# Attention with x regrouped through HBM for its transposition, values loaded in merged transfers, and the loop over the batches written out

## The reference

```python
x = x + tanh(g_xattn[0]) * xattn(layernorm(x), ctx, Wq, bq, Wk, bk, Wv, bv, Wo, bo)
x = x + tanh(g_ffn[0]) * ffn(layernorm(x), W1, b1, phases, w_real, w_imag, W2, b2)

def xattn(x1, x2, ...):                     # 16 heads, softmax over the 77 rows of the context
    q, k, v = x1 @ Wq.T + bq, x2 @ Wk.T + bk, x2 @ Wv.T + bv
    return softmax(q k^T / sqrt(32)) v  @ Wo.T + bo

def ffn(x, ...):                            # 512 -> 2048 -> 512
    h = x @ W1 + b1
    imag = w_imag * sin(phases + 0.1 * h)
    q = h + (cos(phases) * w_real + sin(phases) * w_imag) * imag * 0.1
    return relu(q) @ W2 + b2
```

## Time and profile before

| | |
|---|---|
| time, median of 3 runs | 2233.33 us (2232.54 to 2234.48) |
| the profiled execution | 2231.39 us, span 2229.6 us, mean granted clock 0.995 |
| TensorE busy | 2185.5 us, 98% |
| VectorE, ScalarE, POOL busy | 1445.7 us (65%), 1213.6 us (54%), 408.0 us (18%) |
| transfers | 169.38 MB in 269170 packets, of which 190928 under 512 B |

### The profile page before, as it was taken

One profiled execution on the slowest core, in us unless ns is written; L12 is line 12 of the kernel. 1 busy time (PEld: TensorE's weight loads), 2 busy tenths in 40 slices (PEclk: granted clock), 3 DMA queues, 4 the chain that ended last, 5 costly groups with the idle time before them and its releaser, 6 DMA issues.

```text
span 2229.6 us, 33283 instructions
## 1 busy us (share of the span) xinstructions
PE 2185.5 (98%) x10385; PEld 1826.8 (82%) x10385; DVE 1445.7 (65%) x2596; ACT 1213.6 (54%) x3571; POOL 408.0 (18%) x341
## 2 busy tenths in 40 slices
PE   8989999999999989999999999999999999999999
PEld 6778888888888877888888888888888888888887
DVE  5566776677767747766666566566566666665654
ACT  3477777777767745544454454444544544444444
POOL 5133333333333321101001011011011010110110
PEclk9999999999999999999999999999999999999999
DMA  7513232322232344223123122121231231231210
GB/s 231 180 33 99 79 84 79 102 80 76 86 95 86 84 133 123 67 57 76 57 56 75 56 38 74 51 62 62 51 75 56 56 75 56 56 71 58 40 38 20
DMA packets 269170, 169.38 MB, mean 76 GB/s; under 512 B 190928, under 2 KB 205788, under 8 KB 269066
## 3 DMA queue, kind: packets, MB, share of 16 engines
q1 hardware_dynamic: 267290, 167.63, 27.7%
q0 software_dynamic: 1344, 0.64, 0.2%
q10 hardware_dynamic: 432, 0.04, 0.0%
HBM read 108.86 MB, written 59.38 MB: 75 GB/s over the span
## 4 chain that ended last, share of the span: by engine, by line
PE 61%; DVE 1%; ACT 1%; issue 0%; ACTq 0%
PE m_bank L56 31%; PE pair_bank L56 31%; DVE w_split L1346 0%; DVE hidden L1379 0%; DVE turns L1375 0%; ACT relu L1306 0%; ACT hidden L1315 0%; ACT turns L1317 0%; DVE sine L1372 0%; DVE stats L173 0%; DVE relu L1362 0%; DVE x_in L198 0%; ACT sine L1322 0%; ACT L1322 0%; ACT w_split L1302 0%
## 5 line engine op out<-in xcount | busy, mean ns | idle before, releaser
L56 PE MATMUL m_bank<-xT,w_split 128*128 128x512 f32 x3072 | 740.2, 390 | 4.0 <-DVE w_split L1346 4.0
L56 PE MATMUL pair_bank<-w_split,relu 128*128 128x512 f32 x3072 | 738.4, 389 | 3.4 <-DVE relu L1362 3.2
L56 PEld LDWEIGHTS m_bank<-xT,w_split 128*128 128x128 f32 x3072 | 578.2, 188 | 124.7 <-DVE w_split L1346 4.4
L56 PEld LDWEIGHTS pair_bank<-w_split,relu 128*128 128x128 f32 x3072 | 576.2, 188 | 125.3 <-issue 3.6
L1322 ACT ACTIVATE sine<-turns 128x512 f32<-128x512 f32 x256 | 161.8, 632 | 392.2 <-DVE turns L1375 392.2
L998 ACT ACTIVATE exps<-pair_bank,exp_bias 128x77 f32<-128x77 f32 x1024 | 319.3, 365 | 65.7 <-DVE exp_bias L1044 65.5
L1306 ACT ACTIVATE relu<-hidden 128x512 fp32r<-128x512 f32 x256 | 161.8, 632 | 331.1 <-PE m_bank L56 231.1
L1362 DVE SCALAR_TENSOR_TENSOR relu<-hidden,relu 128x512 fp32r<-128x512 f32 x256 | 181.7, 710 | 201.0 <-ACT relu L1306 201.0
L1379 DVE SCALAR_TENSOR_TENSOR hidden<-sine,sine_gain,hidden 128x512 f32<-128x512 f32 x256 | 197.2, 770 | 169.9 <-ACT sine L1322 169.9
L193 POOL TENSOR_TENSOR rstd<-var_eps,minus_half 128x4 f32<-128x4 f32 x32 | 38.3, 1197 | 1191.1 <-DVE var_eps L189 1191.1
L998 ACT ACTIVATION_READ_ACCUMULATOR exps<-pair_bank,exp_bias 128x1 f32 x1024 | 252.0, 246 | 0.0
(11 more groups left out here) (117 smaller groups left out, 1931.3 us busy)
## 6 DMA issues: line engine op xcount, KB each, us to landing
x_in<-in_x_dram SPq DMA_DIRECT2D x16, 1024.0 KB, 5.6
residual<-in_x_dram SPq DMA_DIRECT2D x64, 256.0 KB, 2.6
x_scratch<-residual SPq DMA_DIRECT2D x64, 256.0 KB, 2.1
x_in<-x_scratch SPq DMA_DIRECT2D x16, 1024.0 KB, 5.6
residual<-x_scratch SPq DMA_DIRECT2D x64, 256.0 KB, 3.2
out_dram<-residual SPq DMA_DIRECT2D x64, 256.0 KB, 2.1
quad_scratch<-x_in SPq DMA_DIRECT2D x60, 256.0 KB, 5.2
x_in<-quad_scratch SPq DMA_DIRECT2D x60, 256.0 KB, 4.6
```

The source lines that it names most:

```text
L56: mm = pe.matmul(out, stationary(s), moving(m), start=first and n == 0, stop=last and n == len(PASSES) - 1)
```

## The change

1. In attention, x no longer goes over TensorE. `regroup_x`, the same function as in the feed-forward stage, is issued by SP in slot 1 for the next batch: it waits for the normalised x, issues four stores, waits for them, and issues four reads back. It stands behind that slot's key loads and ahead of its output store and its value loads. VectorE waits for the reads in slot 2, behind the third chunk of probabilities, and turns the blocks in four instructions; ScalarE takes the four high parts in slot 2 behind its second exponentials, VectorE the four low parts after the inverse of half 1. The queries in slot 3 wait for these.
2. VectorE normalises at the end of slot 0 instead of in slot 1.
3. SP loads the following x in slot 3, behind x's low parts, instead of in slot 2.
4. Values are stored to HBM by head, with the two group pairs and the two parts beside each other, so that one transfer brings a head's rows for two groups (0 and 2, or 1 and 3): 512 B of source in a row, four runs of 128 B in SBUF. There are 12 value loads in a turn instead of 24, six in slot 0 and six in slot 1, behind the value products of these slots and for the same batch's slots 2 and 3 on.
5. The turns of attention are written out instead of being in a hardware loop.

```diff
-    v_parts = nc.dram_tensor("v_scratch", [B * M, 2, D], F32).ap()
+    v_parts = nc.dram_tensor("v_scratch", [B * M, 2 * HG, 2 * G // 2, DH], F32).ap()
...
-        v_diag = sb(att, "v_diag", [P, G, 2, NC, P], F32R)
+        v_diag = sb(att, "v_diag", [P, 2, G // 2, 2, NC, P], F32R)
...
-        def load_values(queue, b, g, loaded):
-            for j, c, p0, m0, n in pieces[g % 2]:
-                cols = slice(g * P + j * DH, g * P + (j + 1) * DH)
-                queue.dma_start(v_diag[p0:p0 + n, g, :, c, j * DH:(j + 1) * DH].bitcast(F32),
-                                v_parts[bass.ds(M * b + m0, n), :, cols]).then_inc(loaded, 16)
+        def load_values(queue, b, second, loaded):
+            for j, c, p0, m0, n in pieces[second]:
+                queue.dma_start(v_diag[p0:p0 + n, second, :, :, c, j * DH:(j + 1) * DH]
+                                .rearrange("p g s d -> p (g s) d").bitcast(F32),
+                                v_parts[bass.ds(M * b + m0, n), HG * second + j]).then_inc(loaded, 16)
...
-                with eng.Fori(2, B - 3, 2) as b:
-                    turn(b, 0, MIDDLE)
-                    turn(b + 1, 1, MIDDLE)
-                turn(B - 2, 0, MIDDLE)
+                for b in range(2, B - 1):
+                    turn(b, b % 2, MIDDLE)
...
             def _(sp):
+                def regroup_x(b):
+                    sp.wait_ge(normed, NT * (b + 1))
+                    for c in range(QUADS):
+                        sp.dma_start(quads[c], x_in[:, :, :].rearrange("p t (k c j) -> p (t k) c j", c=QUADS, j=BLOCK)[:, :, c, :])\
+                          .then_inc(quads_stored[c], 16)
+                    for c in range(QUADS):
+                        sp.wait_ge(quads_stored[c], 16 * b)
+                    for c in range(QUADS):
+                        sp.dma_start(x_in[c * BLOCK:(c + 1) * BLOCK, :, :],
+                                     quads[c].rearrange("(a i) n j -> i a (n j)", i=BLOCK)).then_inc(quads_loaded, 16)
...
-                        if g == 2 and place != AFTER:
-                            sp.wait_ge(t_full, s.x[1][0])
-                            if isinstance(b, int) and b + 2 >= B:
+                        if g == 1 and place != AFTER:
+                            regroup_x(b + 1)
+                        if g == 3:
+                            sp.wait_ge(x_split, KT * (b + 1))
+                            if b + 2 >= B:
                                 load_x(x1_tiles[b + 2 - B])
                             else:
                                 load_x(x_tiles[b + 2])
                         if s.output:
                             store_y(s.output[0], s.output[1], s.output[2])
-                        if s.finish and place != AFTER and not (place == LAST and g >= 2):
+                        if s.finish and place != AFTER and g < 2:
                             sp.wait_ge(m_full, s.values[0])
-                            load_values(sp, s.back[0] + 1, s.back[1], values_loaded[s.back[1]])
+                            load_values(sp, b, g, values_loaded[g])
...
                         if s.queries:
                             if g == 3:
-                                pe.wait_ge(t_split, x_split)
+                                pe.wait_ge(x_split, KT * (b + 1))
                             queries(parity ^ (g == 3), (g + 1) % G, *s.queries[:2])
...
-                        if s.x:
-                            for i in range(2):
-                                transpose_x(2 * (g - 1) + i, *s.x[i], b + 1)
-                            x_split = s.x[1][0]
...
                         if s.x:
-                            for i in range(2):
-                                bank_hi(xT[1 - parity][0][:, 2 * (g - 1) + i, :], *s.x[i])
+                            act.wait_ge(blocks_turned, QUADS * (b + 1))
+                            for kt in range(KT):
+                                act.activation(quad_order(xT[1 - parity][0][:, kt, :]), x_quads[:, :, :, kt, :], ACT.Copy)\
+                                   .then_inc(x_hi_ready, 1)
...
                         if g == 0 and place != AFTER:
                             sums(dve, b + 2, range(NT // 2))
-                        if g == 1 and place != AFTER:
-                            normalise(dve, b + 2)
+                        if g == 2 and place != AFTER:
+                            dve.wait_ge(quads_loaded, 16 * QUADS * (b + 1))
+                            for a in range(QUADS):
+                                dve.transpose(x_in[:, a, :], x_in[:, a, :]).then_inc(blocks_turned, 1)
                         if s.score:
                             inverse(unit + 1, 0)
...
                         if s.x:
-                            for i in range(2):
-                                kt = 2 * (g - 1) + i
-                                bank_lo(xT[1 - parity][1][:, kt, :], xT[1 - parity][0][:, kt, :], *s.x[i])
+                            for kt in range(KT):
+                                dve.wait_ge(x_hi_ready, KT * b + kt + 1)
+                                dve.tensor_tensor(quad_order(xT[1 - parity][1][:, kt, :]), x_quads[:, :, :, kt, :],
+                                                  quad_order(xT[1 - parity][0][:, kt, :].bitcast(F32)), ALU.subtract)\
+                                   .then_inc(x_split, 1)
+                        if g == 0 and place != AFTER:
+                            normalise(dve, b + 2)
                         if s.finish and not s.values_first:
                             heads_lo(parity ^ (g < 2), s.back[1], *s.values[1:])
```

More of the change, by code:

```diff
@@ L232, in gated_attention_ffn_kernel @@
         k_diag = sb(att, "k_diag", [P, G, 2, GC], F32R)
-        v_diag = sb(att, "v_diag", [P, G, 2, NC, P], F32R)
+        v_diag = sb(att, "v_diag", [P, 2, G // 2, 2, NC, P], F32R)
         cleared = sem(whole, "cleared")
         keys_loaded = [sem(whole, f"keys_loaded{g}") for g in range(G)]
-        values_loaded = [sem(whole, f"values_loaded{g}") for g in range(G)]
+        values_loaded = [sem(whole, f"values_loaded{i}") for i in range(2)]
         first_keys_loaded = sem(whole, "first_keys_loaded")
@@ L258, in load_keys, with by_head, part @@
                   .then_inc(loaded, 16)
-        def load_values(queue, b, g, loaded):
-            for j, c, p0, m0, n in pieces[g % 2]:
-                cols = slice(g * P + j * DH, g * P + (j + 1) * DH)
-                queue.dma_start(v_diag[p0:p0 + n, g, :, c, j * DH:(j + 1) * DH].bitcast(F32),
-                                v_parts[bass.ds(M * b + m0, n), :, cols]).then_inc(loaded, 16)
+        def load_values(queue, b, second, loaded):
[3 more added lines that the diff above has]
+                                v_parts[bass.ds(M * b + m0, n), HG * second + j]).then_inc(loaded, 16)
+        def by_head(row):
+            return row.rearrange("p (g h d) -> p g h d", g=G // 2, d=DH)
+        def part(pair, s):
+            return pair.rearrange("p h (g s) d -> p g h s d", s=2)[:, :, :, s, :]
         def setup():
@@ L277, in setup @@
                 v_sum = [sb(st, f"v_sum{j}", [P, D]) for j in range(RT)]
-                v_pair = [sb(st, f"v_pair{j}", [P, 2, D], F32R) for j in range(RT)]
+                v_pair = [sb(st, f"v_pair{j}", [P, 2 * HG, G, DH], F32R) for j in range(RT)]
                 work = [sb(st, f"phase_work{i}", [P, FT]) for i in range(4)]
@@ L403, in _ @@
                         pool.wait_ge(v_stored[j], 16)
-                    for g in range(G):
-                        load_values(pool, 0, g, first_values_loaded)
+                    for second in range(2):
+                        load_values(pool, 0, second, first_values_loaded)
                 @block.tensor
@@ L520, in values_hi @@
                         n = v_rows(j)
[L521 removed]
+                        act.activation(part(v_pair[j][0:n, :, :, :], 0), by_head(v_sum[j][0:n, :]), ACT.Copy)\
+                           .then_inc(v_hi, 1)
                     row = 0
@@ L693, in attention @@
             bo_rows = sb(st, "bo_rows", [P, D])
+            quads_stored = [sem(st, f"quads_stored_a{c}") for c in range(QUADS)]
+            quads_loaded = sem(st, "quads_loaded_a")
+            blocks_turned = sem(st, "blocks_turned_a")
+            x_hi_ready = sem(st, "x_hi_ready")
+            x_split = sem(st, "x_split")
             t_full = sem(st, "t_full_a")
@@ L748, in slots_of @@
                     s.probs = {c: t.next() for c in s.chunks} if s.finish else None
-                    s.x = [t.next() for _ in range(2)] if g in (1, 2) and place != AFTER else None
+                    s.x = g == 2 and place != AFTER
                     s.queries = None
@@ L880, in _ @@
             def _(pe):
-                def transpose_x(kt, n, bank, b):
-                    if kt == 0:
-                        pe.wait_ge(normed, NT * (b + 1))
-                    if not (isinstance(n, int) and n <= 2):
-                        pe.wait_ge(t_split, n - 2)
```

(4 more changed lines are left out.)

21 lines of the change are left out of this document (11 added, 10 removed).

## The result

The changed kernel takes 2332.18 us (median of 4 runs, 2331.24 to 2336.23) against 2232.93 before: a ratio of 1.045, 95% interval 1.0438 to 1.0462. That is 99 us more. The profiled execution took 2331.24 us.

The account below looks back on a forecast made before the run. TensorE bounds attention before; afterwards a closed loop over SP's queue makes the period 52.6 us against 43.2. Attention's 124.6 plus the first turn's 5.7, +130 on 2231.4, gave 2364 us; range 2298 to 2425, the forecast's own 2335 to 2410.

Parts of the forecast that it names:

- The closed loop over SP's queue: Attention: slot 0's product, values, keys, regrouping, transposes, slot 2's product set the period, 52.6 us; stores start at 9.0.
- I take 5.6: SP's queue in attention: issuing slot 0's six merged value loads takes 5.6 us, between bounds of 5.1 and 10.2.
- The round trip, 14.9: Attention's regrouping of x: 9.0 us from first store to first read, then 5.9 us; blocks there at 23.9.
- One idle stretch of 8 us with the lower clock after it: TensorE idles about 8 us before slot 2's value product; the granted clock then drops near half, costing 2.3 us.
- Slot 3, "10.12": Attention's slot 3 on TensorE was counted at 10.12 us within the new period.
- The normalisation, "1.9", and x's low parts, which were to end at about 30.5: VectorE in attention: normalisation takes 1.9 us; ScalarE and VectorE finish x's parts about 30.5 us after slot 1 starts.
- rival A: Attention's regrouping is hidden, blocks landing by 16 before VectorE asks, so no stall arises: 2205 us; chance 0.06.
- Turn-backs, -19.0: Attention's hardware loop written out: five turn-backs at 3.8 us go, saving 19.0 us.
- TensorE's transposes, -28.6: Attention's slots 1 and 2: 16 transposes of x per turn go, 1.8 us over 16 turns, saving 28.6 us.
- B: Regrouping in attention: each pass lands in 5.6 us, round trip 11.2, period 48.9, so 2305 us; chance 0.10.
- D: SP's queue in attention: merged values double their issue time, adding 4.6 x 15, so 2433 us; chance 0.12.
- C: TensorE in attention: the clock stays at 2.4 GHz through the stalls, so 2327 us; chance 0.12.

Follow-up runs that it names:

- first hold: Against the kernel with the regrouping first in SP's slot 1: POOL waits with its second probabilities of slot 0 until x is normalised; 2276.41 us.
- regrouping first: Against the changed kernel: in slot 1 SP issues the regrouping first, then slot 0's six value loads, then the residual and the keys; 2304.92 us.
- normalisation back: Against the changed kernel: VectorE normalises in slot 1 again, behind the peaks, instead of at the end of slot 0; 2346.37 us.
- values unmerged: Against the changed kernel: values in the old layout with 24 loads a turn, six behind each slot's value product; 2377.66 us.
- without the trip: Against the changed kernel: attention's regrouping transfers left out, VectorE turns the normalised blocks in place, so x enters the queries in another order; 2297.66 us.
- loop of four turns: Against the kernel before: four turns in a pass of attention's loop instead of two, so two turn-backs instead of five; 2226.84 us.

## Why the prediction came out as it did

The direction, the place and the mechanism held: 2364 forecast, 2332 measured, inside the stated range, 3 us below the forecast's own. Of +130 us, +99 came. That it came so near is in part luck, since two errors ran against each other. Step by step:

- *The closed loop over SP's queue.* Held. Its length follows the moment at which x's stores start. Put the measured start in place of the prediction's 9.0, at 16 us for each us as in its rivals, and compare:

  | kernel | stores start, us into slot 1 | the prediction's sum with it | measured |
  |---|---|---|---|
  | first hold | 2.2 | 2255 | 2276 |
  | regrouping first | 4.1 | 2286 | 2305 |
  | changed | 5.8 | 2313 | 2332 |
  | normalisation back | 6.4 | 2322 | 2346 |
  | values unmerged | 8.5 | 2356 | 2378 |

  The measured time is 19 to 24 us above the sum each time, though the kernels differ in more than this start. So the loop and its slope are right, all other terms together were about 20 us too low, and the start of the stores was 51 us too high; the difference is the 31 or 32 us between forecast and result.
- *"I take 5.6" for six merged value loads.* Failed, and it is the largest mis-sized term. They took 2.56: a load's issue is 0.40 us (median) merged and 0.82 unmerged. I had bounded it from below by the unmerged loads' time, with no row that excluded less. With two tenths less for the residual and the keys the stores started at 5.8 instead of 9.0.
- *The round trip, 14.9.* Too short by 1.4: 9.06 to the first read, then 7.3 instead of 5.9 until VectorE starts. The reads were not slowed by the other transfers in attention; I had misread. 4.6 us is the median landing of all four reads of a regrouping, and the trip ends with the fourth. In the feed-forward stage of the kernel before the fourth lands 5.3 to 5.9 us after its issue, where the row that I used gives 15.7 us for the trip; in attention after 5.2 to 6.8, with a median of 5.6. The blocks were there at 22.1 instead of 23.9, and a turn of 50.4 instead of 52.6 over 15 turns is the whole of the miss.
- *One idle stretch of 8 us with the lower clock after it.* This sign failed in its size. What was to release whom came as forecast: VectorE stands before its block transposes for the regrouped x, TensorE before slot 2's value product for the queries' low part, and ScalarE no longer waits on issue. In the changed kernel there are two stretches in a turn, one of 2.6 us and one of 1.8 to 4.6, because slot 1's wait and its late peaks make VectorE reach the blocks at 19.5 us instead of 15 to 16. The single stretch of 8 appeared when the normalisation was moved back. The 2.3 us for the clock is too much for such stretches: behind slot 1's it fell in 8 turns of 14.
- *Slot 3, "10.12".* Mis-sized: 11.2 us on average. VectorE is late there after x's low parts, and the slot gets up to 1.8 us longer.
- *The normalisation, "1.9", and x's low parts, which were to end at about 30.5.* Mis-sized: they take 3.8 us, and 4.6 us where 0.68 each would make 2.7. I took durations from places where POOL is idle. The longer normalisation runs beside the trip in the changed kernel and is not on its path; with slot 3's waits it is what was wrong with rival A, which priced VectorE's lateness at 1.3 us a turn.
- *Rival A, 2205 us if the trip is hidden.* No kernel here came to it: without the trip 2298, and with the normalisation moved as well 2229.
- *Turn-backs, -19.0.* Mis-sized: one row multiplied by five; all five sum to -12.1. The prediction's own rows could have said so: 658.5 us for 15 periods, less 15 x 43.21 and with its 2.75 for the second turn added, leaves 13.1. The error is in rival A only; the 2364 starts from the measured 658.5. The 1.8 us by which the feed-forward stage gets longer was not foreseen.
- *TensorE's transposes, -28.6.* The kernel without trip shows the 0.9 us a slot (slot 2: 10.6), but VectorE's work takes more in slot 3.
- *Rivals B and D* were on the wrong side: the trip was not shorter, and merging halved the issue time instead of doubling it. *C*, with its 2327, lies nearer to the result than the forecast does, but by chance: the clock did fall, behind more than half of slot 1's stalls.

## What to carry to other kernels

Draw the closed loop before pricing a transfer: what the issuing queue must first wait for and issue, the trip, and what is queued behind the engine that waits for it. Work taken off the busiest engine pays only if the engine that gets it has room in that very slot. Take durations from rows where the same neighbours are busy, and the landing of the last transfer of a group from the last ones, not from the median of all. Sum all instances of a stall instead of multiplying one, and leave a lower bound open where no row closes it. Test a loop at several lengths: a time that is right at one of them can hide two errors.

## What the runs showed of the hardware

- Merging four 128 B runs that are contiguous in HBM halved a transfer's issue time on SP (0.82 to 0.40 us, median) although its elements doubled. Behind the regrouping's reads six such loads took 4.8 to 5.6 us, and 2.7 us in the same place when the regrouping was left out.
- Of four reads of 256 KB issued one behind the other, the first landed 3.2 to 3.8 us after its issue and the fourth 5.3 to 5.9 (15 regroupings in the feed-forward stage of the kernel before).
- A normalising instruction of VectorE of 0.54 us took up to 1.52 us while POOL worked on float32 tensors in SBUF, and never more than 0.55 when POOL was held. x's low parts took at most 0.69 us with no POOL instruction beside them and up to 1.78 with one.
- Writing out 12 turns of one loop made an unedited loop later in the program 0.8 us a turn longer (87.84 against 87.04), with waits on issue; with the merged values it was 0.7 (87.74). With the loop of four turns it did not get longer (87.02), and in the changed kernel, whose turns are written out as well, by 0.1 only (87.17). The cause stays open.
- After idle stretches of 2.6 us of TensorE, all of one length, the granted clock fell to 0.50 in 8 of 14 turns of the changed kernel and stayed at 1.00 in 6; the nine matmuls of a value product then took up to 3.9 us, or 2.3. After the 15 stretches of 6.6 us and more with the normalisation moved back it had fallen every time.
